# Second attention's loop: the four value products of a group as one block of the next group, with one more row of max scores ahead of it

## What is computed

```python
scores = jnp.einsum('bhqd,bhkd->bhqk', q, k) / math.sqrt(HD)
scores = jnp.where(causal, scores, -jnp.inf)
aw = jax.nn.softmax(scores, axis=-1)
...
aw = aw.reshape(Bx, NQ, 2, Sx, Sx)
aw = aw[:, :, 0] - lam * aw[:, :, 1]
attn = jnp.einsum('bhqk,bhkd->bhqd', aw, v) * (1.0 - LAMBDA_INIT)
```

## Time and profile before

| | us |
|---|---|
| runs shown | 614.96, 609.89, 614.98 (median 614.96) |
| the profiled execution's own time | 612.89 |
| its span | 611.1 |
| PE busy in the span | 510.2 (83%) |
| DVE busy | 425.6 (70%) |
| ACT busy | 335.5 (55%) |
| POOL busy | 311.1 (51%) |

### The profile page before, as it was taken

How to read it: one execution, slowest core, us unless ns; L and a number is a source line. 1 busy time by engine, 2 the same in 40 slices (tenths; PEclk the granted TensorE clock), 3 DMA queues, 4 the chain that set the end, 5 groups by cost and what they waited for, 6 DMA issues and landing times. The chain is left out here.

```text
span 611.1 us, 12837 instructions
## 1 busy us (share of the span) xinstructions
PE 510.2 (83%) x3886; PEld 358.0 (59%) x3886; DVE 425.6 (70%) x1656; ACT 335.5 (55%) x559; POOL 311.1 (51%) x472
## 2 busy tenths in 40 slices
PE   4978559967688999999999999998463699999970
PEld 2657459953355444444544544444362599999970
DVE  4785646646679899999999999945528445454536
ACT  4745336623654677777777777786241354545423
POOL 3541055327553685665685667555200477777630
PEclk9998669988699899999999999999855599999995
DMA  9400112322653545566435444231371111111205
GB/s 324 191 2 18 51 40 70 68 74 63 139 101 91 113 94 127 129 139 136 123 107 130 100 117 96 76 65 38 142 244 45 31 44 50 48 49 49 49 30 204
DMA packets 90496, 58.20 MB, mean 95 GB/s; under 512 B 72673, under 2 KB 76770, under 8 KB 88614
## 3 DMA queue, kind: packets, MB, share of 16 engines
q1 hardware_dynamic: 81550, 41.18, 26.7%
q0 software_dynamic: 3744, 7.68, 4.9%
q10 hardware_dynamic: 5136, 8.52, 4.0%
HBM read 37.72 MB, written 19.63 MB: 94 GB/s over the span
## 5 line engine op out<-in xcount | busy, mean ns | idle before, releaser
L1703 DVE CUSTOM_DVE_ANT_1 banks<-banks,a_mask 128x480 f32<-128x480 f32 (+14 forms) x480 | 190.0, 459 | 14.9 <-PE banks L1960 13.2
L1839 ACT ACTIVATE a_prob_<-banks 128x1024 f32<-128x1024 f32 x160 | 154.9, 1022 | 47.9 <-PE banks L1974 47.9
L1541 POOL TENSOR_SCALAR_AFFINE_SELECT a_prob_<-a_prob_ 128x512 f32<-128x512 f32 x128 | 80.8, 635 | 74.6 <-ACT a_prob_ L1839 73.6
L1960 PE MATMUL banks<-a_k_u_,a_q_u_ 72*128 72x512 bf16 (+15 forms) x512 | 103.0, 291 | 4.3 <-DVE a_neg_max_ L1703 4.1
L1960 PEld LDWEIGHTS banks<-a_k_u_,a_q_u_ 72*128 72x128 bf16 x512 | 64.7, 148 | 67.1 <-DVE a_neg_max_ L1703 34.8
L1191 PE MATMUL banks<-f_hgt,f_w_now 128*112 128x128 f32 (+1 forms) x808 | 102.9, 280 | 0.0
L952 POOL DMA_INDIRECT f_hg<-scratch_h_rows,r_source x62 | 59.8, 964 | 77.0 <-DVE r_source L292 47.8
L1974 PE MATMUL banks<-a_q_u_,a_k_x_ 75*128 75x512 bf16 x320 | 97.9, 387 | 0.7 <-ACT a_prob_ L1839 0.7
L1191 PEld LDWEIGHTS banks<-f_hgt,f_w_now 128*112 128x112 f32 (+1 forms) x808 | 97.6, 187 | 0.0
L1986 PE MATMUL banks<-a_prob_,a_v_g_ 128*32 128x512 f32 (+3 forms) x1024 | 83.7, 444 | 0.4 <-POOL a_prob_ L1541 0.4
L1703 DVE DVE_READ_ACCUMULATOR2_ANT a_neg_max_<- 128x1 f32 x512 | 72.1, 143 | 0.0
(11 more groups left out here) (240 smaller groups left out, 676.9 us busy)
## 6 DMA issues: line engine op xcount, KB each, us to landing
a_q_u_<-scratch_q_parts SPq DMA_DIRECT2D x15, 576.0 KB
scratch_o_rows<-a_o_sb_ ACTq DMA_DIRECT2D x28, 256.0 KB, 2.3
w<-in_w SPq DMA_DIRECT2D x2, 2048.0 KB, 10.3
w<-in_w SPq DMA_DIRECT2D x2, 1792.0 KB, 9.9
scratch_q_parts<-a_part_ SPq DMA_DIRECT2D x24, 128.0 KB
a_k_u_<-scratch_k_parts SPq DMA_DIRECT2D x48, 48.0 KB
scratch_h_rows<-r_h SPq DMA_DIRECT2D x8, 256.0 KB, 2.0
f_back<-scratch_back_rows SPq DMA_DIRECT2D x4, 512.0 KB, 5.1
```

Of the source, the lines that this page charges most:

```text
L1541: nc.gpsimd.affine_select(out=block_p, in_=block_p, pattern=[[0, JH], [1, P]], compare_op=ALU.is_ge, fill=0.0, base=0, channel_multiplier= ...
L1703: last = nc.vector.tensor_tensor_reduce(out=found, in0=found, in1=mask[:, :, TG - 4 * (t + 1):], scale=-1.0, scalar=-MASKED, op0=ALU.add, ...
L1839: nc.scalar.activation(prob[g % 2][:, 2 * e:2 * e + 2].rearrange("p s j t c -> p (s j) t c"), PS[:, b0:b0 + 2, :].rearrange("p s (j c t) - ...
L1960: last = nc.tensor.matmul(PS[:, a % 3, off:off + width], queries[:, g % 2, :, t], k_u[r][:, :, g % 2 * TG:g % 2 * TG + 4 * (t + 1)], start ...
```

## The change

In the loop of PE's queue the first key block's product no longer follows its own group's row 5: it stands, with the other three, in a block of the next group. That block now comes after row 2 instead of row 1. Only the last group keeps its first product where it was. Number and shape of all instructions stay, and DVE's, ACT's and SP's queues and POOL's work are the same as before.

```diff
                 scores(g, 0)
                 rows(0)
                 scores(g, 1)
-                rows(1)
+                rows(1, 2)
                 if g >= 1:
-                    for kb in range(1, NQ):
+                    for kb in range(NQ):
                         values(g - 1, kb)
-                rows(2)
+                rows(3)
                 scores(g, 2)
-                rows(3, 4)
+                rows(4)
                 if g > GROUPS - 3:
                     second_projection(g - (GROUPS - 2))
                 scores(g, 3)
                 rows(5)
-                values(g, 0)
+                if g == GROUPS - 1:
+                    values(g, 0)
```

## The result

The changed kernel takes 643.77 us in the median (641.65 to 649.04, four runs) against 612.84 us before (609.89 to 614.98): a ratio of 1.0513, with an interval of 1.0475 to 1.0551. The prediction was 634.0 us with a range of 627 to 643: the sign and the chain in the loop came out, the time lies 0.8 us beyond the range. The profiled execution is the longest of the four, 649.04 us with a span of 647.3.

The account below looks back on a forecast made before the run. PE was taken as the bound, DVE close behind, coupled by three banks. The profiled 612.9 us plus 19.1 in groups 3 to 28, 0.5 at the end and 1.9 for one clock fall gave 634 us, range 627 to 643.

Parts of the forecast that it names:

- The chain by three banks: Groups 3 to 28: DVE runs out of queued rows during the block, so the period is 7.89 us instead of 7.06.
- the wait before 416: DVE, out of work behind the block of value products, waits 1.31 us for row 3, the 416-column piece.
- that before 384: DVE waits 0.15 us for row 4, which PE writes after the third pair of scores.
- the block of 2.29: PE's four value products in one block of 1280 columns a tile take 2.29 us.
- DVE's share of 84%: DVE's busy share in groups 3 to 28 falls from 95% to some 84%.
- PE's wait before row 2: PE waits some 0.6 us for DVE to free the bank of row 8, ahead of the 448-column row.
- PE's saving: One block less saves PE 0.28 us a group, lost in waiting for DVE; rival keeping the gain: 606 us, chance 0.03.
- ACT's chain, the rival of 613: Rival: ACT's exponentials and the score banks set the loop's pace, period stays 7.06 us, no change, 613 us; chance 0.07.
- The groups with `factors`: Groups 11, 19 and 27: DVE's 1.78 us of `factors` falls in the new gap, period 8.07 us.
- The clock: PE's granted clock falls to half once, lengthening a block of four value products by 1.9 us; bounds allow three more falls.
- The rival of a clock falling often: Rival: the clock falls again and again in the loop, 649 us if every three groups, 682 if every group; chance 0.08.
- Groups 1 and 2: The two groups before the regular stretch were taken at no change, with bounds of -0.4 to +1.5 us.

## Why the prediction was right in the loop and wrong in the time

**The chain by three banks: right, to the hundredth.** Period 7.89 forecast, 7.88 to 7.91 measured in the 21 groups without a fall. Its parts stand in the rows of after: the wait before 416 of 1.31 (1.29 on DVE's row, 1.43 from the last read's start against 3.13 - 1.68 = 1.45), that before 384 of 0.15 (0.16 from the read at 336.51 to 336.67), the block of 2.29 (2.30), going in and row 2 of 0.34 (332.92 to 333.26, 0.34), DVE's share of 84% (82% with the falls, 85% of the kernel with the wait filled).

PE's wait before row 2, given as some 0.6, is 0.51, and that this is near is luck: the terms given for it (four pairs of scores 1.80, rows 1.53, from 3.38 to 7.95) leave 1.24. From row 4 to the end of row 1's 0.21 us PE was held 331.99 + 0.21 - (336.25 - 7.90) = 3.85 us, not 3.33, so the wait is some 0.7 from start to start, of which the profile lists 0.51.

Three other kernels came within 0.06 us of the period that the same walk gave for them (7.46 and 7.50 with one block, 7.20 and 7.26 with other rows, 7.89 with one filling matmul). Two did not: the one with one row ahead (7.06 for 7.55), where a wait was left out of the walk, and the one with two filling matmuls (7.89 for 8.03), which last longer than the wait. The periods expected of the two kernels with the fifth pair moved came from PE's work and from a rough range, not from this walk.

**PE's saving: right that it is lost.** The Trainium skill, TensorEngine Tiling (Array Packing), section Tiling Modes, speaks of a drain at each change of the tiling mode. The trace agrees: row 2, 0.20 us by its columns, holds PE 0.34 us in front of the block. One block less does save PE time, 2.30 us in place of 1.43 + 1.00 for the products alone; it comes out as PE's wait for DVE. ACT's chain, the rival of 613, does not bind: the long wait on ACT is its copy's, 2.6 us a group, for the block to end.

**The groups with `factors`: too dear by 0.18 each.** The step was 1.78 us for `factors`, hence 8.07. DVE in group 11 of after:

```profile
291.72 0.94 DVE L1716 RECIPROCAL a_r_b<-a_l_b_ 128x128 f32<-128x128 f32 x1
292.70 0.63 DVE L1717 TENSOR_SCALAR a_r_b<-a_r_b,a_coef_p 128x128 f32<-128x128 f32 x1
293.25 0.69 DVE L1703 CUSTOM_DVE_ANT_0 banks<-banks,a_mask 128x512 f32<-128x512 f32 x1
...
295.06 0.62 DVE L1703 CUSTOM_DVE_ANT_1 banks<-banks,a_mask 128x416 f32<-128x416 f32 x1
```

They took 293.25 - 291.72 = 1.53 us. By the same walk row 0 starts at 1.35, the rows 0 to 2 end at 3.21, row 3 is ready, row 4 comes at 3.80 as elsewhere, and the period is 7.89; so it was measured, and `factors` vanishes wholly in the gap. That takes 0.5 us off the sum. Why the second instruction was shorter than before was not tried.

**The clock: the step that failed.** The prediction said: "I take one fall, +1.9". This term was too small: there were five in groups 3 to 28 in either profile, at 1.55 each. With that alone the sum is 632.5 + 7.8 = 640.3, which would still lie in the range. The second profile's execution took 640.16; that it agrees to a tenth is luck, since its groups 1 and 2 took 2.3 us more than before and what lies ahead of them 1.5 us less. The median of 643.77 lies 3.5 above the sum. Which stretches hold that at the median is not known, as only two executions were profiled; the slower one has its rest outside groups 3 to 28, 4.9 us of it in group 0 at half clock, for which the prediction had no term. That it is the clock at the median too is borne out by the kernel with one filling matmul: the same period of 7.89, no fall in groups 3 to 28, and 643.77 - 634.18 = 9.6 us less.

The size of one fall was too high, since the clock is back (352.00) before the block ends (352.88); their number was too low. The argument against many of them was that a wait of 0.6 us "is short beside the 5.6 us between two blocks". That was no row, only a comparison of two lengths, and the earlier trace rows did not bear it out either: the fall there came after a stretch in which PE counted as busy for 2.45 of 3.10 us, with two short waits on DVE in it:

```profile
198.21 0.44 PE L1960 MATMUL banks<-a_k_u_,a_q_u_ 72*128 72x288 bf16 x2 [0.32 <-DVE a_neg_max_ L1703]
198.98 0.47 PE L1960 MATMUL banks<-a_k_u_,a_q_u_ 72*128 72x256 bf16 x4 [0.32 <-DVE a_neg_max_ L1703]
```

A wait of 0.51 us in front of each block is of that kind. The Trainium skill, TensorE: Matmul & The Clock Gate, section A second HAM failure mode: psum-queue depth-cycling, tells of another kernel of this kind: it cycles through PSUM banks, lets PE idle briefly between groups of matmuls, and its clock went back and forth. The trace agrees, with five groups of 26, and the two kernels with the wait filled show it from the other side. What no run here settles is why it is five and not all 26: the wait is 0.50 to 0.51 in each. It is not chance, as far as two profiles go, since the falls have the same spacing in both.

**The range.** The rival of a clock falling often (643 to 682, 0.08) was priced for a fall in every third group or more. Up to three more falls than one were put into the bounds, and nothing stood between four falls and nine. The five falls lie in that hole, and the time of 643.77 just inside this rival's bounds: it came true in a milder form than it was priced. How its terms come to the upper bound is not shown: 634 + 5.7 + 2 gives 641.7 and 639 + 2 gives 641, not 643.

**Groups 1 and 2.** They were taken at no change, with +1.5 as the bound. They took 1.8 and 2.3 us more in the two profiles, and 0.9 more with one filling matmul, each time with part of the stretch at half clock. How much of that is the clock and how much the chain was not taken apart.

## What to carry to other kernels

When work is moved so that two stretches without new data become one, compare the longer stretch with what the consumer has queued at that moment, by the number of buffers, and look up which consumer step frees the buffer that the "one ahead" needs: here it was the row just finished, so that being ahead bought nothing. The order of the items in a ring can be worth nearly as much as their place: here rows that keep the consumer longest, put into the buffers before the gap, gave back 0.63 of 0.83 us. And a new wait on TensorE of half a microsecond in every round is to be priced with several falls of the clock, not with one (here five in 26 rounds); cheap filling work in the wait shows how much of a loss it is.

## What the runs showed of the hardware that was not expected

The granted clock fell from 1.00 to 0.50 at a recurring wait of 0.50 to 0.51 us, in a stretch where PE counts as busy for 94%, five times in 26 groups in both profiles, at distances of 40.96 us and once 64.85 or 64.86 us, and not once in the kernels in which 0.60 or 1.03 us of unread matmuls stood in that wait. Adding work that nobody reads made the changed kernel faster by 8 to 10 us. At the start of the loop the clock stood at 0.50 for up to 24 us in some executions (from 188.17 to 212.06 in the first profile of after, from 186.44 to 203.50 in the kernel with the early scores and other rows), in the second of these with PE counted as busy throughout, and in another execution of the changed kernel group 0 ran at 1.00; what decides that stays open.
